# A branch on the number of chosen experts ahead of the loop over further experts

## The chip, the core and the metric

The kernel runs on one core of one Trainium2 chip. A core has a matrix engine (PE), a vector engine (DVE), an activation engine (ACT), a general engine (POOL) and an engine that here only starts transfers (SP). Each has its own instruction stream, and they meet through semaphores alone. The metric is the device time of one execution in microseconds; the comparison is made on the median of several executions.

## The reference

The input has 2 x 512 tokens of 1024 values. A first block adds a quantised product with a context. A second block, a mixture of experts with a shared expert, follows. Cut to what matters here:

```python
scores = softmax(xt @ router_w + router_b) + router_bias      # 1024 tokens x 16 experts
g = scores.reshape(T, 4, 4)
_, gidx = top_k(g.max(axis=-1), 2)                            # the 2 best groups of 4
masked = where(keep(gidx), g, -inf).reshape(T, 16)
_, idx = top_k(masked, 2)                                     # the 2 best experts of a token
gate = zeros((T, 16)).at[arange(T)[:, None], idx].add(vals)   # vals: the scores chosen
for e in range(16):
    h = silu(xt @ ew1[e] + eb1[e]) * (xt @ ew2[e] + eb2[e])   # 1024 -> 256
    y += gate[:, e:e+1] * (h @ ew3[e] + eb3[e])               # 256 -> 1024
z = silu(xt @ sw1 + sb1) * (xt @ sw2 + sb2) @ sw3 + sb3       # the shared expert, 1024 -> 512 -> 1024
x = x + tanh(g_ffn) * (y + z)
```

`xt` is the normalised token. `router_bias` is drawn once from the seed and multiplied by 6.017. Worked out from the reference's `setup_inputs()`, its 16 values are, group by group:

```
group 0 (experts 0 to 3)     -3.742    3.759   10.121   -4.862
group 1 (experts 4 to 7)    -14.238    5.391    8.802   -3.583
group 2 (experts 8 to 11)     7.276    8.880  -10.495   -2.829
group 3 (experts 12 to 15)   -4.648   -5.839   12.613    1.406
```

## The kernel before

All 1024 tokens stay in SBUF as 8 tiles of 128 tokens (`X`, `NT = 8`), transposed in `XT`, as a high and a low f16 part. Every product is made of three f16 products (high x high, high x low, low x high). The program does the quantised product first, then the shared expert, then the router, which finds out on the chip which experts any token chose: `nexp` holds their number, `EL` their indices, `sel` a one-hot row for each place in that list. Each engine reads `nexp` into a register with `chosen(engine)` (line 242).

Two of the chosen experts (`SLOTS = TOPK = 2`) are always there and have code of their own, written out: `expert_up` for 8 units (line 1325, two 128-row pieces of 256 x two halves of the tokens x two experts), whose results go through ACT (`eu_silu`, line 594), POOL (`gate_unit`, line 425, multiplication with the gate), DVE (`eu_gate`, line 872, which counts up `eu_hf`) and again ACT and DVE (high and low part, `eu_hi`, `eu_lo`, line 878). DVE also adds bias rows to `X` (`finish_rows`, lines 890 to 892).

If more than two experts were chosen, a loop `Fori(SLOTS, n)` takes the further ones, with register `a` from 2 to n - 1. It stands in each engine's code. One turn of it:

- SP reads the expert's index from `EL`, loads two bias columns, a bias row, the up weights in 8 pieces and the down weights (lines 312 to 328). It enters the loop only when `w3_lo`, `rows_fin` and `eu_hf >= 8` are reached.
- DVE makes the gate column from `sel[a]`, splits it into two f16 parts and builds diagonal matrices (lines 847 to 1058). PE turns them into gate rows (line 1338). ACT and DVE split the weights (lines 578, 860).
- PE does the up product, 192 matmuls (line 1349), unit by unit with ACT, POOL and DVE (lines 639, 435, 1067, 642, 1071), then the down product, 96 matmuls in 8 tiles (line 1362). DVE adds each tile into `X` (lines 1080, 1082). All of them wait for `xd_read` at the end of a turn.

The loop has its test at its end: the counter is raised and compared after the body. After it PE does the down products of the two fixed experts, and for the second half of the tokens those of the shared expert (`tile_down`, line 1385, 288 matmuls); DVE adds them to `X` (`tile_out`, line 901) and SP writes each tile out (line 368).

The order of work is the order in which the code is written, engine by engine; no scheduler is involved. On PE, line 1333 waits for `eu_hf >= 8` ahead of the loop; ACT waits there for `eu_done >= 8`. DVE and POOL go from `chosen` straight to the loop. The list index `a` beyond the number of chosen experts finds no one-hot row in `sel`, so the gate column is zero there.

Of the kernel before, what the change touches and what calls it, by code (L numbers as in the profile page):

```python
# [5 lines left out]
ALU = mybir.AluOpType  # L6
ACT = mybir.ActivationFunctionType
AX = mybir.AxisListType.X

P = 128  # L10
# [28 lines left out]
def build(nc, x, ctx_in, g_xattn, g_ffn, x1_scale, x1_zp, x2_scale, x2_zp, router_w, router_b, router_bias,  # L39
# [5 lines left out]
    with es:  # L45
# [200 lines left out]
        def _(sp):  # L246
# [59 lines left out]
            def expert_of(j):  # L306
                return sp.value_load(EL[0:1, bass.ds(j, 1)], min_val=0, max_val=E - 1)
# [40 lines left out]
            sp.wait_ge(w3_lo, 2 * SLOTS)  # L348
            sp.wait_ge(rows_fin, NT)
            sp.wait_ge(eu_hf, 8)  # L350
            with sp.Fori(SLOTS, n) as a:
                e = expert_of(a)
                sp.wait_ge(xw3_lo, 2 * a - 4)
                sp.sem_inc(further, 1)
                sp.wait_ge(xd_read, 8 * a - 16)
                sp.sem_inc(further, 1)
                load_bias_columns(e, SLOTS, xb_in)
                load_row(e, 1, xb_in)
                for q in range(4):
                    load_up_quarter(e, q, xw_in[q])  # L360
                sp.wait_ge(xw_lo, 4 * a - 4)
                sp.sem_inc(further, 1)
                load_down(e, 0, xw3_in)

            for i in range(NT):
                if i < NT - 1:
# [11 lines left out]
        def _(pool):  # L378
# [48 lines left out]
            for u in range(8):  # L427
                gate_unit(u)
            n = chosen(pool)
            with pool.Fori(SLOTS, n) as a:  # L430
                pool.wait_ge(xg_rdy, 2 * a - 2)
                pool.sem_inc(further, 1)
                for u in range(4):
                    pool.wait_ge(xu_silu, 4 * a - 8 + u + 1)
                    nc.gpsimd.tensor_tensor(SA[:, u % 2, :], SA[:, u % 2, :], GR[:, 0, u // 2, :], ALU.mult)\  # L435
                        .then_inc(xu_gated, 1)

        @block.scalar
        def _(act):  # L440
# [184 lines left out]

            n = chosen(act)
            act.wait_ge(eu_done, 8)
            with act.Fori(SLOTS, n) as a:
                act.wait_ge(xd_done, 8 * a - 16)
                act.sem_inc(further, 1)  # L630
                for q in range(4):
                    split_up_quarter(xw_in[q], 32 * a - 32, xw_hi, 0, q)
                for b in range(B):
                    gate_rows(b, xg_done, 2 * a - 4 + b + 1, GR[:, 0, b, :], xg_rdy)
                act.wait_ge(xb_in, 48 * a - 48)
                act.sem_inc(further, 1)
                for u in range(4):
                    act.wait_ge(xu_done, 4 * a - 8 + u + 1)
                    nc.scalar.activation(SA[:, u % 2, :], PS[:, 4 + 2 * (u % 2), :], ACT.Silu,
                                         bias=ebc[:, SLOTS, 0, u % 2:u % 2 + 1], scale=1.0 / UPS).then_inc(xu_silu, 1)  # L640
                    act.wait_ge(xu_hf, 4 * a - 8 + u + 1)
                    nc.scalar.activation(HX[:, 0, u % 2, u // 2 * S:(u // 2 + 1) * S], SA[:, u % 2, :], ACT.Copy,
                                         scale=HS / UPS).then_inc(xu_hi, 1)
                    act.wait_ge(xu_lo, 4 * a - 8 + u + 1)
                    act.sem_inc(further, 1)
                act.wait_ge(xw3_in, 16 * a - 16)
                for q in range(HC):
                    nc.scalar.activation(W3X[:, 0, q, :], W3F[0][:, q, :], ACT.Copy, scale=WS).then_inc(xw3_hi, 1)

        @block.vector
        def _(dve):
# [387 lines left out]
                    finish_rows(i)  # L1040

            n = chosen(dve)
            with dve.Fori(SLOTS, n) as a:
                count = [0]

                def linked(ins):

                    count[0] += 1
                    ins.then_inc(x_chain, 1)
                    dve.wait_ge(x_chain, XLINKS * a - SLOTS * XLINKS + count[0])  # L1050

                gate_column(SLOTS, sel[:, bass.ds(a, 1), :], linked)
                ins = split_gates(slice(SLOTS, SLOTS + 1), linked)
                ins.then_inc(xg_split, 1)
                dve.wait_ge(xg_split, a - 1)
                for h in range(2):
                    for b in range(B):
                        v.tensor_tensor(DGX[:, h, b, :, :], idh[:, :].unsqueeze(1).to_broadcast([P, TB, P]),
                                        gsp[:, h, SLOTS, b * TB:(b + 1) * TB].unsqueeze(2).to_broadcast([P, TB, P]),
                                        ALU.mult).then_inc(xg_diag, 1)  # L1060
                for q in range(4):
                    low_quarter(xw_hi, 4 * a - 8 + q + 1, 0, q, xw_lo)
                dve.wait_ge(xb_in, 48 * a - 48)
                linked(v.tensor_scalar(ebu[:, SLOTS, :], ebc[:, SLOTS, 1, :], UPS, None, ALU.mult))
                for u in range(4):
                    dve.wait_ge(xu_gated, 4 * a - 8 + u + 1)
                    v.scalar_tensor_tensor(SA[:, u % 2, :], PS[:, 5 + 2 * (u % 2), :], ebu[:, SLOTS, u % 2:u % 2 + 1],  # L1067
                                           SA[:, u % 2, :], ALU.add, ALU.mult).then_inc(xu_hf, 1)
                    dve.wait_ge(xu_hi, 4 * a - 8 + u + 1)
                    ts = slice(u // 2 * S, (u // 2 + 1) * S)  # L1070
                    v.scalar_tensor_tensor(HX[:, 1, u % 2, ts], SA[:, u % 2, :], HS / UPS, HX[:, 0, u % 2, ts], ALU.mult,
                                           ALU.subtract).then_inc(xu_lo, 1)
                for q in range(HC):
                    dve.wait_ge(xw3_hi, 2 * a - 4 + q + 1)
                    v.scalar_tensor_tensor(W3X[:, 1, q, :], W3F[0][:, q, :], WS, W3X[:, 0, q, :], ALU.mult,  # L1075
                                           ALU.subtract).then_inc(xw3_lo, 1)
                for i in range(NT):
                    Xi = X[:, i, :].rearrange("p (h n) -> p h n", h=2)
                    dve.wait_ge(xd_done, 8 * a - 16 + i + 1)
                    linked(v.scalar_tensor_tensor(Xi, PS[:, 2 * (i % 2):2 * (i % 2) + 2, :], cf[:, 11:12], Xi, ALU.mult,  # L1080
                                                  ALU.add))
                    v.scalar_tensor_tensor(X[:, i, :], B3[1], tgate[:, SLOTS, i:i + 1], X[:, i, :], ALU.mult, ALU.add)\  # L1082
                        .then_inc(xd_read, 1)
                dve.wait_ge(xd_read, 8 * a - 8)
                assert count[0] == XLINKS

            for i in range(NT):
                tile_out(i)
# [3 lines left out]
        def _(pe):  # L1092
# [238 lines left out]

            n = chosen(pe)
            pe.wait_ge(eu_hf, 8)
            with pe.Fori(SLOTS, n) as a:
                pe.wait_ge(xg_diag, 4 * a - 4)
                for b in range(B):
                    for h in range(2):
                        last = mm(PS[:, b, :], onesh[:, :], DGX[:, h, b, :, :].rearrange("p t n -> p (t n)"),
                                  start=(h == 0), stop=(h == 1))
                    last.then_inc(xg_done, 1)  # L1340
                pe.wait_ge(xw_lo, 4 * a - 4)
                for u in range(4):
                    if u >= 2:
                        pe.wait_ge(xu_hf, 4 * a - 8 + u - 1)
                    for w in range(2):
                        cs = slice(w * INTER + u % 2 * P, w * INTER + (u % 2 + 1) * P)
                        for k in range(KC):
                            for m, (wp, xp) in enumerate(((0, 0), (0, 1), (1, 0))):
                                last = mm(PS[:, 4 + 2 * (u % 2) + w, :], W12S[0][:, wp, k, cs],  # L1349
                                          XT[:, xp, k, u // 2 * S:(u // 2 + 1) * S], start=(k == 0 and m == 0),  # L1350
                                          stop=(k == KC - 1 and m == 2))
                    last.then_inc(xu_done, 1)
                pe.wait_ge(xu_lo, 4 * a - 4)
                pe.wait_ge(xw3_lo, 2 * a - 2)
                pe.wait_ge(xg_rdy, 2 * a - 2)
                for i in range(NT):
                    if i >= 2:
                        pe.wait_ge(xd_read, 8 * a - 16 + i - 1)
                    for h in range(2):
                        for c in range(HC):  # L1360
                            for m, (hp, wp) in enumerate(((0, 0), (1, 0), (0, 1))):
                                last = mm(PS[:, 2 * (i % 2) + h, :], HX[:, hp, c, i * P:(i + 1) * P],  # L1362
                                          W3X[:, wp, c, h * 512:(h + 1) * 512], start=(c == 0 and m == 0),
                                          stop=(c == HC - 1 and m == 2))
                    last.then_inc(xd_done, 1)
                pe.wait_ge(xd_read, 8 * a - 8)

            def tile_down(i):

# [50 lines left out]
```

## Time and profile before

| | us |
|---|---|
| median of 3 runs (lowest, highest) | 428.83 (427.85, 429.19) |
| the profiled execution: its own time | 426.34 |
| its span, first to last instruction | 424.5 |
| PE busy / DVE busy / ACT busy / POOL busy | 372.4 / 227.6 / 119.3 / 40.9 |
| mean granted TensorE clock | 0.964 of full speed |

The span is 1.84 us shorter than the profiled execution's own time, and that is 2.49 us below the median of the three timed runs. PE is busy for 88% of the span, and the core's 16 DMA engines move 90 GB/s in the mean. Read the table of stages first, then the queue instructions of the loop's lines, and only then the groups by line: the program has one stage whose work depends on the data.

### The profile page before, as it was taken

How to read it: one execution, taken by the hardware profiler on the slowest of the kernel's cores; microseconds unless marked ns; L12 is line 12 of the kernel's file. 1: busy time of each engine (PE TensorE's matmuls, PEld its weight loads, DVE VectorE, ACT ScalarE, POOL GpSimd, SP SyncE). 2: the span in 40 equal slices, each digit the busy share in tenths (PEclk: the TensorE clock that was granted, in tenths of full speed). 3: DMA queues.
4: the chain of work that ended last, by engine and by line, in shares of the span. 5: the costliest groups of instructions: out<-in, count | busy, mean ns of one | idle time of the engine just before them, and what ended most of it. 6: DMA issues, size and time to landing. Idle time of an engine off the chain costs nothing.

```text
span 424.5 us, 5372 instructions
## 1 busy us (share of the span) xinstructions
PE 372.4 (88%) x2191; PEld 181.9 (43%) x2191; DVE 227.6 (54%) x371; ACT 119.3 (28%) x133; POOL 40.9 (10%) x45
## 2 busy tenths in 40 slices
PE   0697998999999999999999993179993897999996
PEld 0343896444446444444444441024441342444442
DVE  4778879679845677245434898521112595221111
ACT  3893675882431116321231111221113000000000
POOL 2101101001300053011111111001111000000000
PEclk9999999999999999999999998569999798999999
DMA  8991504980560029250000000820000000121111
GB/s 305 379 314 28 171 30 135 236 300 0 100 148 2 2 78 323 96 198 2 0 0 2 0 0 2 247 99 2 2 0 0 0 2 1 63 111 59 60 56 49
DMA packets 37125, 38.19 MB, mean 90 GB/s; under 512 B 16740, under 2 KB 31084, under 8 KB 37100
## 3 DMA queue, kind: packets, MB, share of 16 engines
q1 hardware_dynamic: 37088, 37.85, 28.7%
q8 instruction: 17, 0.28, 0.3%
q14 instruction: 8, 0.07, 0.0%
q10 hardware_dynamic: 12, 0.00, 0.0%
HBM read 30.50 MB, written 4.19 MB: 82 GB/s over the span
## 4 chain that ended last, share of the span: by engine, by line
PE 62%; DVE 16%; issue 13%; ACT 3%; DMA 3%; POOL 2%; SPq 1%; ACTq 0%; POOLq 0%; DVEq 0%
PE PS L1385 15%; PE PS L1164 15%; PE PS L1325 15%; PE PS L1111 5%; PE PS L1199 5%; PE PS L1362 4%; DVE stats L666 3%; DMA ring<-in_L_ffn_ew_dram 1%; DVE areaW L720 1%; DVE X L891 1%; DVE X L1082 1%; DVE X L1080 1%; DVE X L890 1%; POOL SA L435 1%; DVE X L892 1%
## 5 line engine op out<-in xcount | busy, mean ns | idle before, releaser
L1164 PE MATMUL PS<-areaT,areaW 128*128 128x512 f16 x288 | 62.7, 379 | 1.4 <-DVE SA L751 1.4
L1349 PE MATMUL PS<-areaT,area 128*128 128x512 f16 x192 | 43.8, 393 | 8.3 <-DVE area L860 8.3
L1164 PEld LDWEIGHTS PS<-areaT,areaW 128*128 128x128 f16 x288 | 27.9, 98 | 35.0 <-DVE SA L751 1.6
L1325 PE MATMUL PS<-areaT,area 128*128 128x512 f16 x192 | 41.6, 379 | 0.0
L1325 PE MATMUL PS<-areaT,areaW 128*128 128x512 f16 x192 | 41.6, 379 | 0.0
L901 DVE SCALAR_TENSOR_TENSOR X<-PS,cf,X 128x512 f32<-128x512 f32 x16 | 12.0, 751 | 53.2 <-PE PS L1385 53.2
L1349 PEld LDWEIGHTS PS<-areaT,area 128*128 128x128 f16 x192 | 19.3, 101 | 33.3 <-DVE area L860 9.2
L1111 PE MATMUL PS<-area,areaQ 128*128 128x512 f16 x128 | 31.2, 395 | 0.3
L1362 PE MATMUL PS<-areaW 128*128 128x512 f16 x96 | 23.4, 404 | 8.3 <-DVE areaW L1075 7.9
L1325 PEld LDWEIGHTS PS<-areaT,areaW 128*128 128x128 f16 x192 | 18.8, 98 | 22.6
L1325 PEld LDWEIGHTS PS<-areaT,area 128*128 128x128 f16 x192 | 18.8, 98 | 22.6
L1385 PE MATMUL PS<-areaW,rows 128*128 128x512 f16 x96 | 22.6, 400 | 3.0 <-DVE X L1082 3.0
L1067 DVE SCALAR_TENSOR_TENSOR SA<-PS,ebu,SA 128x512 f32<-128x512 f32 x4 | 3.0, 752 | 39.5 <-POOL SA L435 39.5
L398 POOL TENSOR_TENSOR lnR<-lnV,mhalf 128x1 f32<-128x1 f32 (+1 forms) x13 | 13.4, 1034 | 100.3 <-DVE lnV L669 100.3
L666 DVE BATCH_NORM_STATS2 stats<-X 128x6 f32<-128x512 f32 x32 | 20.5, 683 | 4.2 <-DMA X<-in_x_dram 4.0
L1385 PE MATMUL PS<-SW,areaH 128*128 128x512 f16 x96 | 22.0, 379 | 0.0
L1385 PE MATMUL PS<-areaW,QI 128*128 128x512 f16 x96 | 22.0, 379 | 0.0
L1199 PE MATMUL PS<-SW,areaH 128*128 128x512 f16 x96 | 20.9, 379 | 0.0
L872 DVE SCALAR_TENSOR_TENSOR SA<-PS,ebu,SA 128x512 f32<-128x512 f32 x8 | 6.0, 748 | 25.8 <-POOL SA L425 25.8
L425 POOL TENSOR_TENSOR SA<-SA,areaQ 128x512 f32<-128x512 f32 x8 | 10.9, 1367 | 87.1 <-ACT SA L594 87.1
L1111 PEld LDWEIGHTS PS<-area,areaQ 128*128 128x128 f16 x128 | 12.4, 100 | 15.6 <-DVE area L703 1.3
L1362 PEld LDWEIGHTS PS<-areaW 128*128 128x128 f16 x96 | 9.3, 103 | 22.3 <-DVE areaW L1075 8.4
(174 smaller groups left out, 464.2 us busy)
## 6 DMA issues: line engine op xcount, KB each, us to landing
ring<-in_L_ffn_sw_dram SPq DMA_DIRECT2D x12, 512.0 KB, 5.0
ring<-in_L_ffn_ew_dram SPq DMA_DIRECT2D x24, 256.0 KB, 5.5
X<-in_x_dram SPq DMA_DIRECT2D x8, 512.0 KB, 6.2
areaT<-in_ctx_dram SPq DMA_DIRECT2D x8, 512.0 KB, 10.1
ring<-in_ctx_dram SPq DMA_DIRECT2D x8, 512.0 KB, 3.8
out_dram<-X SPq DMA_DIRECT2D x7, 512.0 KB, 2.6
ring<-in_L_ffn_ew_dram SPq DMA_DIRECT2D x3, 1024.0 KB, 4.9
B3b<-in_L_ffn_eb_dram SPq DMA_DIRECT2D x2, 512.0 KB, 6.2
```

Of the source, the lines that this page charges most:

```text
L398: nc.gpsimd.tensor_tensor(lnR[:, lo:lo + n], lnV[:, lo:lo + n], mhalf[:, 0:n], ALU.pow)\
L425: nc.gpsimd.tensor_tensor(SA[:, u % 2, :], SA[:, u % 2, :], GR[:, j, b, :], ALU.mult).then_inc(eu_gated, 1)
L666: ins = v.bn_stats(stats[:, i, 6 * h:6 * h + 6], X[:, i, h * 512:(h + 1) * 512])
L872: v.scalar_tensor_tensor(SA[:, u % 2, :], PS[:, EU_BANK[u] + 1, :], ebu[:, j, u % 2:u % 2 + 1], SA[:, u % 2, :], ALU.add, ALU.mult).then_i ...
L901: v.scalar_tensor_tensor(X[:, i, hs], PS[:, pb + h, :], cf[:, 11:12], X[:, i, hs], ALU.mult, ALU.add)\
L1111: mm(PS[:, AT_BANK[i] + h, :], Q1T[:, i % TB, k, :], Q2[:, k, h * 512:(h + 1) * 512], start=(k == 0), stop=False)
L1164: last = mm(PS[:, SU_BANK[half * SC + c] + w, lo:hi], SW[:, wp, 2 * c + w, k, :], XT[:, xp, k, tk], start=(k == 0 and n == 0), stop=(k == ...
L1199: last = mm(PS[:, pb + h, :], HT[:, hp, c, i * P:(i + 1) * P], SW3[:, wp, c, hs], start=(c == 0 and n == 0), stop=(c == SC - 1 and n == 2))
L1325: last = mm(PS[:, EU_BANK[u] + w, :], W12S[j][:, wp, k, cs], XT[:, xp, k, b * S:(b + 1) * S], start=(k == 0 and n == 0), stop=(k == KC - 1 ...
L1349: last = mm(PS[:, 4 + 2 * (u % 2) + w, :], W12S[0][:, wp, k, cs], XT[:, xp, k, u // 2 * S:(u // 2 + 1) * S], start=(k == 0 and m == 0), st ...
L1362: last = mm(PS[:, 2 * (i % 2) + h, :], HX[:, hp, c, i * P:(i + 1) * P], W3X[:, wp, c, h * 512:(h + 1) * 512], start=(c == 0 and m == 0), s ...
L1385: last = mm(PS[:, DN_BANK[i] + h, :], ht[:, hp, q, ts], w3[:, wp, c, hs], start=(s == 0 and m == 0), stop=(s == len(parts) - 1 and m == 2))
```

## The change

On each of the five engines the loop is put inside an `If(n > SLOTS)`. Nothing in the loop's body, ahead of it or behind it is changed. The same edit on PE, SP, POOL, ACT and DVE (`...` stands for the body, which is only indented):

```diff
@@ sync
             sp.wait_ge(w3_lo, 2 * SLOTS)
             sp.wait_ge(rows_fin, NT)
             sp.wait_ge(eu_hf, 8)
-            with sp.Fori(SLOTS, n) as a:
-                e = expert_of(a)
...
+            with sp.If(n > SLOTS):
+                with sp.Fori(SLOTS, n) as a:
+                    e = expert_of(a)
...
@@ gpsimd
             n = chosen(pool)
-            with pool.Fori(SLOTS, n) as a:
-                pool.wait_ge(xg_rdy, 2 * a - 2)
...
+            with pool.If(n > SLOTS):
+                with pool.Fori(SLOTS, n) as a:
+                    pool.wait_ge(xg_rdy, 2 * a - 2)
...
@@ scalar
             n = chosen(act)
             act.wait_ge(eu_done, 8)
-            with act.Fori(SLOTS, n) as a:
...
+            with act.If(n > SLOTS):
+                with act.Fori(SLOTS, n) as a:
...
@@ vector
             n = chosen(dve)
-            with dve.Fori(SLOTS, n) as a:
...
+            with dve.If(n > SLOTS):
+                with dve.Fori(SLOTS, n) as a:
...
@@ tensor
             n = chosen(pe)
             pe.wait_ge(eu_hf, 8)
-            with pe.Fori(SLOTS, n) as a:
-                pe.wait_ge(xg_diag, 4 * a - 4)
...
+            with pe.If(n > SLOTS):
+                with pe.Fori(SLOTS, n) as a:
+                    pe.wait_ge(xg_diag, 4 * a - 4)
...
```

In PE's instruction stream this is what stands where the loop is entered, before (an ISA row is a register operation; line 1325 is the last up product of the fixed experts, 1338 and 1349 are the loop's body):

```order
L1325 MATMUL PS<-areaT,areaW 128x512 x47
L242 TENSOR_LOAD nexp [waits el_rdy]
L242 ISA x2
L1334 UNCONDITIONAL_BRANCH [waits eu_hf]
L1334 ISA
L1338 MATMUL PS<-areaQ,onesh 128x512 [waits xg_diag]
```

and with the change (each line number of PE is 4 or 5 higher):

```order
L1329 MATMUL PS<-areaT,areaW 128x512 x47
L242 TENSOR_LOAD nexp [waits el_rdy]
L242 ISA x2
L1338 COMPARE_AND_BRANCH [waits eu_hf]
L1339 UNCONDITIONAL_BRANCH
L1339 ISA
L1343 MATMUL PS<-areaQ,onesh 128x512 [waits xg_diag]
```

A compare-and-branch has come in front of the way into the loop. It waits for the same semaphore as the old first instruction there.

Where PE leaves the loop, before (1362 is the body's down product, 1385 `tile_down`):

```order
L1362 MATMUL PS<-areaW 128x512 x11
L1366 REGISTER_ALU
L1334 REGISTER_ALU [waits xd_read]
L1334 COMPARE_AND_BRANCH
L1385 MATMUL PS<-areaW,rows 128x512 [waits w3_lo,eu_lo,eu_hf]
```

and with the change:

```order
L1367 MATMUL PS<-areaW 128x512 x11
L1371 REGISTER_ALU
L1339 REGISTER_ALU [waits xd_read]
L1339 COMPARE_AND_BRANCH
L1338 UNCONDITIONAL_BRANCH
L1390 MATMUL PS<-areaW,rows 128x512 [waits w3_lo,eu_lo,eu_hf]
```

Behind the loop's own test stands the jump to the end of the `If`; `tile_down` is that end.

## Rows read from the trace of the kernel before

**Rows 1.** Stages: busy us and count of each engine, granted clock, DMA share, GB/s

```profile
0.00:258.93 258.93, 239.31 (x1611) 124.37 (x1611) 173.69 (x312) 105.54 (x116) 34.30 (x40) 1.00 0.39 117
258.93:263.04 4.11, 0.00 (x0) 0.00 (x0) 4.04 (x3) 0.69 (x2) 1.51 (x1) 0.97 0.00 0
263.04:278.77 15.73, 1.89 (x4) 0.43 (x4) 9.20 (x15) 5.83 (x7) 0.00 (x0) 0.50 0.59 168
278.77:322.60 43.83, 43.81 (x192) 19.27 (x192) 4.36 (x7) 3.95 (x6) 3.79 (x3) 0.95 0.07 25
322.60:330.51 7.91, 0.00 (x0) 0.00 (x0) 3.81 (x4) 3.32 (x4) 1.26 (x1) 0.82 0.00 0
330.51:357.23 26.72, 23.36 (x96) 9.36 (x97) 20.51 (x16) 0.00 (x0) 0.00 (x0) 0.93 0.00 1
357.23:424.50 67.27, 64.01 (x288) 28.48 (x288) 12.02 (x16) 0.00 (x0) 0.00 (x0) 0.97 0.16 63
```

**Rows 2.** PE's sequencer at line 1334: duration ns min/median/max, first and last start

```profile
L1334 PEldq MOVE  x1: 33/33/33, 263.0 to 263.0; - x1
L1334 PEldq FUSED_REGOPS  x1: 50/50/50, 263.1 to 263.1; - x1
L1334 PEldq ALU_OP  x1: 32/32/32, 356.9 to 356.9; - x1
L1334 PEldq COMPARE_BRANCH  x1: 98/98/98, 357.0 to 357.0; - x1
```

**Rows 3.** Timeline from 255 us: start, us, engine, line, tile, idle and releaser

```profile
262.27 0.74 DVE L872 SCALAR_TENSOR_TENSOR SA<-PS,ebu,SA 128x512 f32<-128x512 f32 x1
263.70 0.69 DVE L878 SCALAR_TENSOR_TENSOR QI<-SA,QI 128x512 f16<-128x512 f32 x1 [0.70 <-ACT QI L600]
```

**Rows 4.** Chain that ended last, where the loop is left: start, us, what

```profile
355.55 1.30 DVE X L1082
356.85 0.38 issue
357.23 64.02 PE PS L1385 x288
421.25 0.02 issue
421.28 0.75 DVE X L901
```

**Rows 5.** The page: busy us and counts; instruction fetches (packets, MB, share of 16 engines)

```profile
PE 372.4 (88%) x2191; PEld 181.9 (43%) x2191; DVE 227.6 (54%) x371; ACT 119.3 (28%) x133; POOL 40.9 (10%) x45
...
q8 instruction: 17, 0.28, 0.3%
q14 instruction: 8, 0.07, 0.0%
```

**Rows 6.** The list of DMAs: count, KB each, us to landing

```profile
ring<-in_L_ffn_ew_dram SPq DMA_DIRECT2D x24, 256.0 KB, 5.5
...
ebc<-in_L_ffn_eb_dram SPq DMA_DIRECT2D x6, 1.0 KB, 2.2
```

**Rows 7.** Stages as in Rows 1, cut where the granted clock changes

```profile
278.77:283.26 4.49, 4.49 (x11) 1.64 (x12) 0.03 (x1) 0.00 (x0) 0.00 (x0) 0.50 0.67 234
330.51:334.46 3.95, 3.95 (x10) 1.47 (x11) 0.00 (x0) 0.00 (x0) 0.00 (x0) 0.50 0.00 0
357.23:358.35 1.12, 1.12 (x6) 0.53 (x7) 0.00 (x0) 0.00 (x0) 0.00 (x0) 1.00 0.02 7
358.35:361.76 3.41, 3.41 (x10) 1.18 (x9) 0.27 (x1) 0.00 (x0) 0.00 (x0) 0.50 0.00 0
```

**Rows 8.** DVE's and SP's sequencers at their loop lines, as in Rows 2

```profile
L1043 DVEq MOVE  x1: 50/50/50, 264.6 to 264.6; - x1
L351 SPq COMPARE_BRANCH  x1: 62/62/62, 279.4 to 279.4; - x1
```

**Rows 9.** Timeline behind the loop: the first evacuation and the first write

```profile
361.49 0.75 DVE L901 SCALAR_TENSOR_TENSOR X<-PS,cf,X 128x512 f32<-128x512 f32 x1 [4.65 <-PE PS L1385]
365.08 0.37 SPq L368 DMA_DIRECT2D out_dram<-X  x1
```

More of the change, by code:

```diff
@@ L350, in _ @@
             sp.wait_ge(eu_hf, 8)
-            with sp.Fori(SLOTS, n) as a:
-                e = expert_of(a)
[L353 to L363, printed above, removed]
+            with sp.If(n > SLOTS):
+                with sp.Fori(SLOTS, n) as a:
+                    e = expert_of(a)
+                    sp.wait_ge(xw3_lo, 2 * a - 4)
+                    sp.sem_inc(further, 1)
+                    sp.wait_ge(xd_read, 8 * a - 16)
+                    sp.sem_inc(further, 1)
+                    load_bias_columns(e, SLOTS, xb_in)
+                    load_row(e, 1, xb_in)
+                    for q in range(4):
+                        load_up_quarter(e, q, xw_in[q])
+                    sp.wait_ge(xw_lo, 4 * a - 4)
+                    sp.sem_inc(further, 1)
+                    load_down(e, 0, xw3_in)
             for i in range(NT):
@@ L429, in _ @@
             n = chosen(pool)
-            with pool.Fori(SLOTS, n) as a:
-                pool.wait_ge(xg_rdy, 2 * a - 2)
[L432 to L436, printed above, removed]
+            with pool.If(n > SLOTS):
+                with pool.Fori(SLOTS, n) as a:
+                    pool.wait_ge(xg_rdy, 2 * a - 2)
+                    pool.sem_inc(further, 1)
+                    for u in range(4):
+                        pool.wait_ge(xu_silu, 4 * a - 8 + u + 1)
+                        nc.gpsimd.tensor_tensor(SA[:, u % 2, :], SA[:, u % 2, :], GR[:, 0, u // 2, :], ALU.mult)\
+                            .then_inc(xu_gated, 1)
         @block.scalar
@@ L627, in _ @@
             act.wait_ge(eu_done, 8)
-            with act.Fori(SLOTS, n) as a:
[L629 to L644, printed above, removed]
-                    act.sem_inc(further, 1)
-                act.wait_ge(xw3_in, 16 * a - 16)
-                for q in range(HC):
-                    nc.scalar.activation(W3X[:, 0, q, :], W3F[0][:, q, :], ACT.Copy, scale=WS).then_inc(xw3_hi, 1)
@@ new lines, in _ @@
+            with act.If(n > SLOTS):
+                with act.Fori(SLOTS, n) as a:
+                    act.wait_ge(xd_done, 8 * a - 16)
+                    act.sem_inc(further, 1)
+                    for q in range(4):
+                        split_up_quarter(xw_in[q], 32 * a - 32, xw_hi, 0, q)
+                    for b in range(B):
+                        gate_rows(b, xg_done, 2 * a - 4 + b + 1, GR[:, 0, b, :], xg_rdy)
+                    act.wait_ge(xb_in, 48 * a - 48)
+                    act.sem_inc(further, 1)
+                    for u in range(4):
+                        act.wait_ge(xu_done, 4 * a - 8 + u + 1)
+                        nc.scalar.activation(SA[:, u % 2, :], PS[:, 4 + 2 * (u % 2), :], ACT.Silu,
+                                             bias=ebc[:, SLOTS, 0, u % 2:u % 2 + 1], scale=1.0 / UPS).then_inc(xu_silu, 1)
+                        act.wait_ge(xu_hf, 4 * a - 8 + u + 1)
+                        nc.scalar.activation(HX[:, 0, u % 2, u // 2 * S:(u // 2 + 1) * S], SA[:, u % 2, :], ACT.Copy,
+                                             scale=HS / UPS).then_inc(xu_hi, 1)
+                        act.wait_ge(xu_lo, 4 * a - 8 + u + 1)
+                        act.sem_inc(further, 1)
+                    act.wait_ge(xw3_in, 16 * a - 16)
+                    for q in range(HC):
+                        nc.scalar.activation(W3X[:, 0, q, :], W3F[0][:, q, :], ACT.Copy, scale=WS).then_inc(xw3_hi, 1)
@@ L1042, in _ @@
             n = chosen(dve)
-            with dve.Fori(SLOTS, n) as a:
[L1044 to L1085, printed above, removed]
@@ new lines, in _, with linked @@
+            with dve.If(n > SLOTS):
+                with dve.Fori(SLOTS, n) as a:
+                    count = [0]
+                    def linked(ins):
+                        count[0] += 1
+                        ins.then_inc(x_chain, 1)
+                        dve.wait_ge(x_chain, XLINKS * a - SLOTS * XLINKS + count[0])
+                    gate_column(SLOTS, sel[:, bass.ds(a, 1), :], linked)
+                    ins = split_gates(slice(SLOTS, SLOTS + 1), linked)
+                    ins.then_inc(xg_split, 1)
+                    dve.wait_ge(xg_split, a - 1)
+                    for h in range(2):
+                        for b in range(B):
+                            v.tensor_tensor(DGX[:, h, b, :, :], idh[:, :].unsqueeze(1).to_broadcast([P, TB, P]),
+                                            gsp[:, h, SLOTS, b * TB:(b + 1) * TB].unsqueeze(2).to_broadcast([P, TB, P]),
+                                            ALU.mult).then_inc(xg_diag, 1)
+                    for q in range(4):
+                        low_quarter(xw_hi, 4 * a - 8 + q + 1, 0, q, xw_lo)
+                    dve.wait_ge(xb_in, 48 * a - 48)
+                    linked(v.tensor_scalar(ebu[:, SLOTS, :], ebc[:, SLOTS, 1, :], UPS, None, ALU.mult))
+                    for u in range(4):
+                        dve.wait_ge(xu_gated, 4 * a - 8 + u + 1)
+                        v.scalar_tensor_tensor(SA[:, u % 2, :], PS[:, 5 + 2 * (u % 2), :], ebu[:, SLOTS, u % 2:u % 2 + 1],
+                                               SA[:, u % 2, :], ALU.add, ALU.mult).then_inc(xu_hf, 1)
+                        dve.wait_ge(xu_hi, 4 * a - 8 + u + 1)
+                        ts = slice(u // 2 * S, (u // 2 + 1) * S)
+                        v.scalar_tensor_tensor(HX[:, 1, u % 2, ts], SA[:, u % 2, :], HS / UPS, HX[:, 0, u % 2, ts], ALU.mult,
+                                               ALU.subtract).then_inc(xu_lo, 1)
+                    for q in range(HC):
+                        dve.wait_ge(xw3_hi, 2 * a - 4 + q + 1)
+                        v.scalar_tensor_tensor(W3X[:, 1, q, :], W3F[0][:, q, :], WS, W3X[:, 0, q, :], ALU.mult,
+                                               ALU.subtract).then_inc(xw3_lo, 1)
+                    for i in range(NT):
+                        Xi = X[:, i, :].rearrange("p (h n) -> p h n", h=2)
+                        dve.wait_ge(xd_done, 8 * a - 16 + i + 1)
+                        linked(v.scalar_tensor_tensor(Xi, PS[:, 2 * (i % 2):2 * (i % 2) + 2, :], cf[:, 11:12], Xi, ALU.mult,
+                                                      ALU.add))
+                        v.scalar_tensor_tensor(X[:, i, :], B3[1], tgate[:, SLOTS, i:i + 1], X[:, i, :], ALU.mult, ALU.add)\
+                            .then_inc(xd_read, 1)
+                    dve.wait_ge(xd_read, 8 * a - 8)
+                    assert count[0] == XLINKS
@@ L1333, in _ @@
             pe.wait_ge(eu_hf, 8)
-            with pe.Fori(SLOTS, n) as a:
-                pe.wait_ge(xg_diag, 4 * a - 4)
[L1336 to L1366, printed above, removed]
@@ new lines, in _ @@
+            with pe.If(n > SLOTS):
+                with pe.Fori(SLOTS, n) as a:
+                    pe.wait_ge(xg_diag, 4 * a - 4)
+                    for b in range(B):
+                        for h in range(2):
+                            last = mm(PS[:, b, :], onesh[:, :], DGX[:, h, b, :, :].rearrange("p t n -> p (t n)"),
+                                      start=(h == 0), stop=(h == 1))
+                        last.then_inc(xg_done, 1)
+                    pe.wait_ge(xw_lo, 4 * a - 4)
+                    for u in range(4):
+                        if u >= 2:
+                            pe.wait_ge(xu_hf, 4 * a - 8 + u - 1)
+                        for w in range(2):
+                            cs = slice(w * INTER + u % 2 * P, w * INTER + (u % 2 + 1) * P)
+                            for k in range(KC):
+                                for m, (wp, xp) in enumerate(((0, 0), (0, 1), (1, 0))):
+                                    last = mm(PS[:, 4 + 2 * (u % 2) + w, :], W12S[0][:, wp, k, cs],
+                                              XT[:, xp, k, u // 2 * S:(u // 2 + 1) * S], start=(k == 0 and m == 0),
+                                              stop=(k == KC - 1 and m == 2))
+                        last.then_inc(xu_done, 1)
+                    pe.wait_ge(xu_lo, 4 * a - 4)
+                    pe.wait_ge(xw3_lo, 2 * a - 2)
+                    pe.wait_ge(xg_rdy, 2 * a - 2)
+                    for i in range(NT):
+                        if i >= 2:
+                            pe.wait_ge(xd_read, 8 * a - 16 + i - 1)
+                        for h in range(2):
+                            for c in range(HC):
+                                for m, (hp, wp) in enumerate(((0, 0), (1, 0), (0, 1))):
+                                    last = mm(PS[:, 2 * (i % 2) + h, :], HX[:, hp, c, i * P:(i + 1) * P],
+                                              W3X[:, wp, c, h * 512:(h + 1) * 512], start=(c == 0 and m == 0),
+                                              stop=(c == HC - 1 and m == 2))
+                        last.then_inc(xd_done, 1)
+                    pe.wait_ge(xd_read, 8 * a - 8)
```

## The prediction

> **What bounds the kernel now.** I read the stages first. Up to 258.93 us PE is busy for 239.31 us at full clock, and after 357.23 us for 64.01 of 67.27 us [rows 1]. Between them lies everything that the diff wraps: 94.19 us from 263.04 to 357.23, with PE busy for 1.89 + 43.81 + 23.36 = 69.06 us and idle for the rest. Its matmul counts are 4, 192 and 96, and that is one turn of the loop (gate rows, up product, down product), no more and no less.
>
> Next come PE's sequencer rows at the loop's line. The counter is set once, at 263.0 us, and the compare-and-branch is passed once, at 357.0 us, behind the body [rows 2]; the chain goes on from there with `tile_down` [rows 4]. In the instruction order of before, no comparison stands ahead of the body: it is entered whatever n is. So one turn in the trace means n = 3, or n = 2 and a turn that nobody asked for. The trace cannot tell these apart; the inputs can.
>
> A score is a softmax value (0 to 1) plus the bias. Group 3's best is at least 12.61. Group 0's is at least 10.12, group 2's at most 8.88 + 1 = 9.88, group 1's at most 8.80 + 1. So each token keeps groups 3 and 0, whatever its logits. In them expert 14 has at least 12.61 and expert 2 at least 10.12, the next (expert 1) at most 3.76 + 1. All 1024 tokens choose experts 14 and 2. The narrowest margin is 0.24, far above f16 rounding. n is 2, and the turn in the trace works with a gate of zero: it reads weights of some expert and adds zeros to X.
>
> **The change, part by part.** With n = 2 the new comparison sends every engine past the loop. What goes is the whole turn: on PE 292 matmuls, on SP its 12 transfers, on ACT, POOL and DVE their share. The body works on tiles that it alone fills (or adds zeros to X), so nothing behind it needs it. The time that goes is not a sum of busy times but the distance between two moments on PE.
>
> *Start of the gap.* PE's last up product ends at 258.93. Its wait for eu_hf >= 8, which stays, is ended by DVE's line 872, 262.27 + 0.74 = 263.01 [rows 3]; PE's sequencer moves at 263.04 [rows 1, 2]. These 4.11 us of idle time remain.
>
> *The branch.* Between the start of the old compare-and-branch (about 356.97; it takes 98 ns) and the first matmul of `tile_down` at 357.23 lie 0.26 us [rows 2, 4]. The same at the new place: 263.04 + 0.26 = 263.30. In the trace that branch falls through, the new one is taken.
>
> *The jump.* The trace has no taken forward jump, so I bound it. The queue of instruction fetches moved 0.28 MB in 17 packets, 16.5 KB each; for 17 packets 0.3% of 16 engines' 424.5 us is 20.4 us, 1.2 us each [rows 5]. PE has 2191 loads and 2191 matmuls [rows 5], so a packet stands for some 257 instructions (4382 / 17). The body has 292 x 2 = 584 plus a few waits: the target lies over two packets ahead. If it is on the engine already, the jump costs about 0. If one packet must be fetched, PE stands still for the way of a small transfer from issue to landing, 2.2 us [rows 6], or up to that plus the packet's own 1.2 us, 3.4 us. Two such fetches one after the other are 6.8 us, my upper end. I take 2.8 us, the middle of one fetch, since the old body ran through by steady fetches and nothing announces the jump. PE then starts again at 263.30 + 2.8 = 266.10.
>
> The Trainium skill bears on this ("Runtime: NRT & Kernel Launch", Instruction fetch mechanics): prefetch is sequential, and "a taken branch whose target isn't in the current 2-page window forces a DMA fetch of the target page". By that rule, with pages of 256 instructions, 584 ahead is a miss; it gives no price. The same section gives TensorE room for 2048 instructions; were all of it filled ahead, there would be no miss. No row here shows which it is, so the jump at no cost is a rival below.
>
> *The tail.* From the first matmul of line 1385 to the end of the span it is 67.27 us [rows 1]. Every wait in it is met earlier or in the same order: eu_hf, eu_lo and w3_lo of the fixed experts are reached by 263.70 + 0.69 = 264.39 [rows 3], and the waits on y_rdy follow DVE's evacuations. DVE reads nexp and comes to its branch at 264.6 [rows 8]; the first result comes 361.49 - 357.23 = 4.26 us after the first matmul [rows 9], about 270.4 now. DVE, whose body is far shorter than PE's, has 5.7 us for its own jump. SP branches at about 263.1 and its first write comes 365.08 - 357.23 = 7.85 us after PE's start [rows 9]; that hides its jump. ACT and POOL have nothing left to do. If this cover were gone, DVE would have 4 tiles of PSUM banks to catch up in.
>
> *The clock.* The tail of before ran at 0.50 (1.2 GHz) for 3.41 us, after an idle time of 3.0 us; the two restarts with over 7 us of idle before them ran at 0.50 for 4.49 and 3.95 us [rows 7, 1]. Now PE idles for 266.10 - 258.93 = 7.2 us. I take the mean of those two, 4.2 us; 0.8 us more at half speed cost 0.4 us. Tail: 67.7 us.
>
> *Sum.* Span 266.10 + 67.7 = 333.8 us, against 424.5: 90.7 less. Against the profiled execution's own time that is 426.34 - 90.7 = 335.6; the median of the timed runs stands 2.49 us higher, 428.83 - 90.7 = 338.1 us. I predict 338.1.
>
> **The rivals.**
>
> *The jump is free.* For it: fetches run ahead in the body without a gap in the matmuls. Against it: the distance, over two packets. PE starts at 263.30, idle for 4.4 us. With the tail at 67.7 the span is 331.0 and the time 335.3. If the clock has not fallen either (in stage 258.93 to 263.04 it was still 0.97 in the mean, so it fell only at its end [rows 1]), the tail loses the half of 3.41 us: 65.6 us, span 328.9, time 333.2.
>
> *The jump is dear.* Two fetches in a row, or one that waits for others: 6.8 us, span 263.30 + 6.8 + 67.7 = 337.8, time 342.1.
>
> *The loop is not skipped, and nothing changes.* This needs n >= 3 in the runs that are timed, other inputs than the ones I worked out, or a chip whose list of experts is longer. The trace would look just as it does. Then the new rows cost two branches per engine on the path, 0.2 us: 429.0. The margins above speak against it.
>
> *Not skipped, and slower.* The same case, with the body left by the new jump at its end (the row behind the loop's test in the order of after). If that one, taken to the very next block, throws away what was fetched ahead, PE stands for one fetch of 2.8 us at 357 us, where nothing covers it: 428.8 + 0.2 + 2.8 = 431.8. It is slower as soon as that jump costs over 1.1 us.
>
> **How the numbers follow.** One fetch at PE's jump (PE back at 265 to 267.5): 0.58, 337 to 339.6, likeliest 338.1. Free jump: 0.27, 333.2 to 336. Dear jump: 0.10, up to 342.1. Not skipped: 0.03 with no change, 0.02 slower. The range of 334.0 to 341.0 leaves out the lowest part of the free jump (0.05), the top of the dear one (0.05) and the 0.05 of not skipped. A measurement of this kernel tells a difference from none at about 0.3%, 1.3 us. Faster 0.95, same 0.03, slower 0.02.
>
> **What would show it.** In the profile after: no instructions at the body's lines and 1899 matmuls in place of 2191; 24 - 8 = 16 transfers of 256 KB of expert weights in place of 24 [rows 6]; PE's compare-and-branch at about 263 us and the first matmul of `tile_down` at 266.1. That distance is the jump's price: 0.3 us means a free jump, 3.1 my forecast, over 5 the dear one. The stage from that matmul to the end should be 67.7 us, and DVE should wait for PE, never PE for DVE, in it. I am wrong if matmuls of the body's lines still appear, if DVE or SP comes out of its own jump later than PE needs it, or if the tail is over 1 us longer than before at the same clock.

## The result and the profile after

| | before | after |
|---|---|---|
| median (lowest, highest), us | 428.34 (426.86, 429.19), 4 runs | 337.41 (337.24, 338.44), 4 runs |
| ratio, 95% interval | 1 | 0.7885 (0.7857 to 0.7914) |
| the profiled execution: time, span | 426.34, 424.5 | 337.24, 335.4 |

The change makes the kernel 90.9 us faster; 338.1 us were forecast, in a range of 334.0 to 341.0. The line numbers of the changed kernel are 1 to 5 higher: 1329 is the last up product of the fixed experts (1325 before), 1390 `tile_down` (1385), 904 `tile_out` (901).

The page of the changed kernel, the same lines as before:

```profile
span 335.4 us, 4614 instructions
...
PE 304.2 (91%) x1899; PEld 154.1 (46%) x1899; DVE 190.1 (57%) x331; ACT 106.8 (32%) x117; POOL 35.9 (11%) x41
...
q8 instruction: 16, 0.26, 0.3%
...
ring<-in_L_ffn_ew_dram SPq DMA_DIRECT2D x16, 256.0 KB, 5.4
```

1899 matmuls in place of 2191 and 16 transfers of expert weights in place of 24 [rows 5, 6]: the whole turn of the loop is gone.

The stages of the changed kernel, cut at the same events as [rows 1] (columns as there; the last up product ends at 260.45, `eu_hf` reaches 8 at 264.57, `tile_down` starts at 268.25, the clock rises at 271.53):

```profile
0.00:260.45 260.45, 240.24 (x1611) 125.60 (x1611) 173.31 (x312) 105.46 (x115) 34.35 (x40) 0.99 0.38 116
260.45:264.57 4.12, 0.00 (x0) 0.00 (x0) 4.04 (x3) 0.69 (x2) 1.50 (x1) 1.00 0.01 2
264.57:268.25 3.68, 0.00 (x0) 0.03 (x1) 0.69 (x1) 0.62 (x1) 0.00 (x0) 0.52 0.03 9
268.25:271.53 3.28, 3.28 (x8) 1.17 (x9) 0.00 (x0) 0.00 (x0) 0.00 (x0) 0.50 0.02 5
271.53:335.40 63.87, 60.65 (x281) 27.30 (x279) 12.01 (x16) 0.00 (x0) 0.00 (x0) 1.00 0.17 66
```

The stages of the loop, 94.19 us from 263.04 to 357.23 [rows 1], have become the 3.68 us of the third row. What PE's sequencer did in it (line 1338, duration in ns):

```profile
L1338 PEldq COMPARE_BRANCH  x1: 3520/3520/3520, 264.6 to 264.6; - x1
```

The old branch, which fell through, took 98 ns [rows 2]. This one is taken and takes 3520. In the same 3.68 us the list of DMAs has one packet on the queue of instruction fetches that is PE's:

```profile
q8 instruction: 1, 0.02, 1.9%
```

1.9% of 16 engines' 3.68 us is 1.1 us of transfer. The packet starts 0.95 us after the branch does, and the branch ends 1.5 us after the packet: most of the 3.5 us is the way of the fetch, not its bytes. The same comparison on DVE (line 1046), one record of its line:

```profile
L1046 DVEq COMPARE_BRANCH  x1: 72/72/72, 266.1 to 266.1; - x1
```

SP's takes 53 ns, ACT's and POOL's 45 ns each. Only PE, whose jump goes over some 600 instructions (a matmul counts as two, its weight load and itself), stands still. And behind the jump (timeline of the changed kernel):

```profile
272.65 0.75 DVE L904 SCALAR_TENSOR_TENSOR X<-PS,cf,X 128x512 f32<-128x512 f32 x1 [6.73 <-PE PS L1390]
...
276.01 0.37 SPq L369 DMA_DIRECT2D out_dram<-X  x1
```

DVE waits for PE (6.73 us), not PE for DVE, and SP's first write comes 7.76 us after PE's start; before it was 7.85 [rows 9].

### The profile page after: what moved, and what is told of

The parts are those of the page before. It is cut to its first block, busy times and chain, and to the rows that moved or that the text cites. A ratio compares the mean times of both kernels' runs of the same rounds, so it can differ in the third digit from the quotient of the medians.

```text
span 335.4 us, 4614 instructions
## 1 busy us (share of the span) xinstructions
PE 304.2 (91%) x1899; PEld 154.1 (46%) x1899; DVE 190.1 (57%) x331; ACT 106.8 (32%) x117; POOL 35.9 (11%) x41
## 4 chain that ended last, share of the span: by engine, by line
PE 76%; DVE 14%; issue 4%; ACT 3%; DMA 1%; POOL 1%; ACTq 0%; DVEq 0%; POOLq 0%
PE PS L1390 19%; PE PS L1168 19%; PE PS L1329 19%; PE PS L1115 7%; PE PS L1203 6%; DVE stats L669 3%; PE PS L1184 3%; DVE X L894 2%; DVE X L893 2%; DVE X L895 1%; DMA sc<-in_g_ffn_dram 1%; PE PS L1122 1%; DVE X L740 1%; POOL lnR L399 1%; DVE SA L875 1%
## 5 line engine op out<-in xcount | busy, mean ns | idle before, releaser
L1168 PEld LDWEIGHTS PS<-areaT,areaW 128*128 128x128 f16 x288 | 27.9, 98 | 35.0 <-DVE SA L754 1.6
L1329 PE MATMUL PS<-areaT,area 128*128 128x512 f16 x192 | 41.6, 379 | 0.0
L1329 PEld LDWEIGHTS PS<-areaT,area 128*128 128x128 f16 x192 | 18.8, 98 | 22.6
L1329 PEld LDWEIGHTS PS<-areaT,areaW 128*128 128x128 f16 x192 | 18.8, 98 | 22.6
L875 DVE SCALAR_TENSOR_TENSOR SA<-PS,ebu,SA 128x512 f32<-128x512 f32 x8 | 6.0, 748 | 25.8 <-POOL SA L426 25.8
L596 ACT ACTIVATE SA<-PS,ebc 128x512 f32<-128x512 f32 x8 | 5.5, 688 | 46.8 <-PE PS L1329 46.8
L1390 PEld LDWEIGHTS PS<-areaW,rows 128*128 128x128 f16 x96 | 9.7, 102 | 20.6 <-issue 10.5
L1184 PE MATMUL PS<-areaT,areaW 128*128 128x128 f16 x256 | 16.4, 229 | 1.2 <-issue 1.2
L1184 PEld LDWEIGHTS PS<-areaT,areaW 128*128 128x128 f16 x256 | 15.8, 103 | 1.4 <-issue 1.3
L487 ACT ACTIVATE rows<-X,lnB,lnA 128x1024 f32<-128x1024 f32 x8 | 9.9, 1239 | 19.9 <-DVE lnB L680 19.9
```

Of the source, the lines that this page charges most:

```text
L487: nc.scalar.activation(rows[:, i % 2, :], X[:, i, :], ACT.Identity, bias=lnB[:, i:i + 1], scale=lnA[:, i:i + 1]).then_inc(ln_xs, 1)
L875: v.scalar_tensor_tensor(SA[:, u % 2, :], PS[:, EU_BANK[u] + 1, :], ebu[:, j, u % 2:u % 2 + 1], SA[:, u % 2, :], ALU.add, ALU.mult).then_i ...
L1168: last = mm(PS[:, SU_BANK[half * SC + c] + w, lo:hi], SW[:, wp, 2 * c + w, k, :], XT[:, xp, k, tk], start=(k == 0 and n == 0), stop=(k == ...
L1184: mm(PS[:, 4 + 2 * c + w, tk], SW[:, 0, 2 * c + w, k, :], XT[:, xp, k, tk], start=(k == 0 and xp == 0), stop=False)
L1329: last = mm(PS[:, EU_BANK[u] + w, :], W12S[j][:, wp, k, cs], XT[:, xp, k, b * S:(b + 1) * S], start=(k == 0 and n == 0), stop=(k == KC - 1 ...
L1390: last = mm(PS[:, DN_BANK[i] + h, :], ht[:, hp, q, ts], w3[:, wp, c, hs], start=(s == 0 and m == 0), stop=(s == len(parts) - 1 and m == 2))
```

## The experiments

All of them were compared with the kernel before on the same chip. Theory A: the gain is the skipped turn, and the only price on the path is PE's jump, which has to fetch its target.

**1. No branch at all.** There is neither loop nor `If` on any of the five engines. Written as an edit of the kernel before (PE's part; `...` stands for the body, which is deleted too):

```diff
-            with pe.Fori(SLOTS, n) as a:
...
```

> The loop and the branch ahead of it are left out on all five engines (right for these inputs, where n is 2; experts beyond two would be missing). Theory A (PE's taken jump over the body fetches its target; nothing else in the branch is on the path): in the profile the gap between eu_hf >= 8 and the first matmul of tile_down falls from 3.68 us to about 0.3, and the time from 337.4 to 334.0. Rival B (the 3520 ns record is a wait or a restart of PE, not the jump): the gap stays at 3 us or more and the time at 337.4.

Measured: 333.96 us (332.34 to 334.65), ratio 0.7792 (0.7739 to 0.7844). Stages of this kernel, up to the end of the up product, the gap, and the rest:

```profile
0.00:259.46 259.46, 239.30 (x1611) 124.43 (x1611) 173.25 (x312) 105.29 (x115) 34.35 (x40) 1.00 0.38 117
259.46:263.63 4.17, 0.00 (x1) 0.01 (x1) 4.08 (x3) 0.71 (x2) 1.50 (x1) 0.92 0.00 0
263.63:330.50 66.87, 63.66 (x288) 28.43 (x288) 12.71 (x17) 0.60 (x1) 0.00 (x0) 0.98 0.16 63
```

The gap is 4.17 us, nearly all of it the wait for `eu_hf`. With the branch it is 4.12 + 3.68 = 7.80. The jump costs 3.6 us by the gaps and 3.4 by the medians, as expected. Rival B is refuted.

**2. No branch on PE alone.** The changed kernel with `If` and loop deleted on PE only.

> The loop and its branch are left out on PE alone; SP, ACT, POOL and DVE keep both (right for n = 2). Theory A: the same time as the kernel without any branch, 334.0 within 0.5, since the four other jumps lie beside PE's work. Rival C (one of the other jumps is as dear and DVE or SP is late for PE or for the writes): over 1 us above it, 335 to 337.4.

Measured: 333.98 us (333.24 to 335.28), ratio 0.7788 (0.7732 to 0.7845), the same as without any branch (333.96). The jumps of the other four engines cost nothing that can be measured, as theory A has it; rival C is refuted.

**3. The wait moved behind the branch.**

```diff
-            pe.wait_ge(eu_hf, 8)
             with pe.If(n > SLOTS):
+                pe.wait_ge(eu_hf, 8)
                 with pe.Fori(SLOTS, n) as a:
```

`tile_down` has waits of its own, so nothing is given up by this.

> PE's wait for eu_hf >= 8 moves from ahead of the branch into the branch's body, so that PE can jump while its queue still holds up products. Theory A (the price is a fetch, which needs only the sequencer): the branch starts at the end of the nexp load, 3.5 us before the queue is empty, the fetch is hidden, tile_down starts within 0.5 us of the last up product, 7.5 us earlier than in the changed kernel, and the clock doesn't fall, 1.6 us more: 328.3. Rival B (the price comes after the queue has run dry, so it can't be hidden): only the 4.1 us of wait go, 333.3.

Measured: 328.42 us (326.94 to 329.95), ratio 0.7665 (0.7604 to 0.7726). The jump is as long as before, but it starts at 256.6 us, while PE still has matmuls in its queue:

```profile
L1337 PEldq COMPARE_BRANCH  x1: 3320/3320/3320, 256.6 to 256.6; - x1
```

Stages of this kernel, as for experiment 1:

```profile
259.73:260.08 0.35, 0.00 (x1) 0.03 (x1) 0.35 (x1) 0.31 (x1) 0.00 (x0) 1.00 0.00 0
260.08:325.60 65.52, 62.32 (x288) 28.08 (x288) 16.36 (x20) 1.00 (x2) 1.52 (x1) 1.00 0.16 65
```

The gap of 7.80 us is 0.35, and the tail is 65.52 us in place of 67.15 (3.28 + 63.87 above), since the clock stays at 1.00 (2.4 GHz). Together 9.1 us, and the medians differ by 9.0. The fetch is still there, one packet on PE's fetch queue between 256.6 and 260.08 us, but it stops the sequencer only: the up products that PE had queued ran on until 259.73 us and covered 3.1 of the jump's 3.3 us.

**4. The jump announced.** A prefetch hint for it two units (96 matmuls) ahead:

```diff
             for u in range(8):
+                if u == 6:
+                    soon = pe.mark_branch_hint_location()
                 expert_up(u)
...
-            with pe.If(n > SLOTS):
+            jump = pe.br_cond(n > SLOTS, on_true="pe_further", on_false="pe_down")
+            jump.branch_hint(soon)
+            with nc.body("pe_further", valid_engines=PE_ONLY):
...
```

> PE's jump is announced: a branch prefetch hint stands two units (96 matmuls) ahead of it. Everything else is the changed kernel. Theory A: if the hint brings the target in beside the sequential fetches, the 3520 ns record falls to about 0.1 us and the time to 334.0. If the stall is no fetch (rival B), or the hint does nothing: 337.4 and a record of 3.5 us.

Measured: 334.26 us (332.26 to 335.65), ratio 0.7778 (0.7721 to 0.7835), and the record of the jump:

```profile
L1343 PEldq COMPARE_BRANCH  x1: 401/401/401, 265.6 to 265.6; - x1
```

**5. The loop entered through the `If`.** The condition is `n > SLOTS - 1` on each engine, so that the turn of zeros is run.

> The branch asks n > SLOTS - 1 on all five engines, so with n = 2 the loop is entered through the If and takes its one turn of zeros. Theory A (the gain is the turn that is skipped and nothing else; an If that is entered costs its few branches): the time of the kernel before, 428.5, within 1.3 us; PE's loop is left through one more jump of about 0.1 us. Rival D (the jump behind the loop's test throws away what was fetched ahead): 428.5 + 3.4 = 431.9.

Measured: 428.71 us (427.14 to 431.09) beside 428.37 of before, ratio 1.0029 (0.9998 to 1.0059). PE's leaving of the loop (duration in ns, start):

```profile
L1339 PEldq COMPARE_BRANCH  x1: 102/102/102, 359.9 to 359.9; - x1
```

The first matmul of `tile_down` follows at 360.18, 0.27 us later, as before (0.26). Rival D's 431.9 us would be a ratio of 1.008, above the interval: it is refuted. A cost of the entered `If` is not shown; the interval leaves room for up to 2.5 us. In the profiled executions the loop's stage is 1.39 us longer than before (95.58 us at a mean clock of 0.83, against 94.19 at 0.86) and the tail 1.65 us shorter (65.62 against 67.27), differences that go with the clock; at the branch itself the rows are as before.

**6 and 7. Shorter bodies.** The body on PE, which isn't run, is made shorter, so that the jump is shorter: an up product over one and over four of the eight row blocks.

```diff
-                            for k in range(KC):
+                            for k in range(1):
```

> In the body that is jumped over, PE's up product has 24 matmuls in place of 192 (right for n = 2, since the body isn't run): 124 matmuls and as many loads, some 262 instructions from jump to target, where the changed kernel has some 600. Theory A1 (what is on the engine is the packet being read and the next one): the target is in the next packet, the record falls to 0.1 us and the time to 334.0. Theory A2 (any taken jump of PE costs 3.5 us): 337.4.

> As the shorter body, with 96 matmuls in the up product: 196 matmuls, some 406 instructions from jump to target. The jump stands some 200 instructions into its packet of 256, so the target is in the second packet after it. Theory A1 (only the packet being read and the next are there): a record of 3.5 us, 337.4. If more than that is fetched ahead (A3): 0.1 us, 334.0.

Measured: 338.02 us (337.21, 338.83), ratio 0.7883 (0.7842 to 0.7923), for some 262 instructions; 338.25 (337.47, 339.04), ratio 0.7888 (0.7848 to 0.7928), for some 406. The two records of the jump, of the shorter and the longer body:

```profile
L1338 PEldq COMPARE_BRANCH  x1: 3297/3297/3297, 264.4 to 264.4; - x1
```

```profile
L1338 PEldq COMPARE_BRANCH  x1: 3880/3880/3880, 265.4 to 265.4; - x1
```

The longer one is as theory A1 has it. It takes 0.4 us more than the changed kernel's because its packet starts 1.46 us after the jump and not 0.95; why is not shown. The shorter one is a miss: A1 expected no stall. Either any taken jump costs this (A2), or my count of where the packets begin was off and its target lies in the second packet after all.

**8. Both edits of 3 and 4.**

> Both edits on PE: the wait moved into the branch's body and the hint two units ahead. Theory A: the fetch is hidden twice over; what the moved wait alone still shows between the last up product and tile_down (0.3 us) can't shrink by more than 0.2 us, so the same time as with the moved wait alone, 328.4, within 1.0. Rival: the hint's early fetch displaces a packet that is still needed, and PE stalls before the jump: 330 or more.

Measured: 327.13 us (326.50 to 328.50), ratio 0.7635 (0.7602 to 0.7668), the fastest version. Its jump starts at 256.7 us and takes 406 ns; the up product runs into `tile_down` without a gap, and the mean clock of the whole execution is 0.999. Against the moved wait alone (0.7665) the intervals overlap, so the hint's own share isn't shown.

**9 and 10. Two very short bodies**: two waits and no matmul; 52 matmuls.

> The shorter bodies (262 and 406 instructions from jump to target) still showed PE's record at 3.3 and 3.9 us, so the distance doesn't decide down to 262. Here PE's loop body holds two waits and no matmul (right for n = 2): the target is about 8 instructions behind the jump, in the same packet. Theory A4 (a taken jump stalls when its target lies outside the packet being read, even in the next one): a record near 0.1 us and 334.0. Theory A2 (any taken jump of PE costs 3.3 us or more): 3.3 us and 337.4.

> PE's loop body has 52 matmuls (right for n = 2): the target is about 111 instructions behind the jump. The fetches of the kernel before place the next packet's boundary some 28 instructions behind the jump, so the target is early in the next packet. A4: a record of 3.3 us, 337.4, as for 262 instructions. A2: the same. If it is instead the distance in instructions (A5: PE's queue holds what is near): 0.1 us, 334.0.

Measured: 334.25 us (333.74, 334.75), ratio 0.7805 (0.7775 to 0.7836), and 334.70 (333.98, 335.41), ratio 0.7816 (0.7774 to 0.7857). The record of the jump is the same in both; that of the body with 52 matmuls:

```profile
L1338 PEldq COMPARE_BRANCH  x1: 365/365/365, 265.3 to 265.3; - x1
```

So not every taken jump stalls (A2 falls), and the next packet is there already (A4 as written falls too). Left are packets (A4') or a reach of some length between 111 and 262 instructions (A5).

**11 and 12. Packet or distance.** The body with 100 matmuls; and the body with 124 that stalled, with the jump shifted against the packets:

```diff
             for u in range(8):
+                if u in (5, 6):
+                    for _ in range(30):
+                        pe.wait_ge(eu_hf, 1)
                 expert_up(u)
```

> PE's loop body has 100 matmuls (right for n = 2): the target is some 207 instructions behind the jump, 96 further than in the run with 52 matmuls (0.37 us, no stall) and 58 nearer than in the one with 124 (3.3 us). Theory A4' (what is on the engine is the packet being read and the next; the jump stands shortly before a boundary, so a target up to some 256 further on is there): a record near 0.37 us, 334.3. Theory A5 (a fixed reach of about 128 instructions): 3.3 us and 337.4.

> The body with 124 matmuls that stalled for 3.3 us, same distance from jump to target, but 60 waits that are met already stand ahead of it in PE's stream (30 each before the sixth and the seventh unit), so that the jump lies early in its packet and the target in the next one in place of the second. Theory A4' (packets decide): a record near 0.37 us and 334.3. Theory A5 (distance decides): 3.3 us again, 337.4. The added waits themselves lie behind PE's queue of matmuls, up to 1 us if they don't.

Measured: 334.19 us (334.16, 334.21), ratio 0.7793 (0.7770 to 0.7816), with a record of 365 ns; and 334.85 (333.89, 335.82), ratio 0.7809 (0.7753 to 0.7865), with this one:

```profile
L1341 PEldq COMPARE_BRANCH  x1: 457/457/457, 265.5 to 265.5; - x1
```

The 60 waits are 30 instructions in PE's stream, since two waits go into one: its trace has 30 semaphore records more than the changed kernel's, 2 of them at line 1322 and 28 at the added line:

```profile
L1336 PEldq EVENT_SEMAPHORE  x28: 51/51/51, 226.2 to 238.0; - x28
```

The body and the distance are those of experiment 6, and the record falls from 3297 to 457 ns because 30 instructions more stand ahead of it. The fetch queue shows why. In experiment 6 no packet moves for PE between 253 and 264 us, and one moves inside the jump. With the shift, one moves between 253 and 256 us, 11 us ahead of the jump:

```profile
q8 instruction: 1, 0.02, 1.8%
```

The distance does not decide; where the packets begin does. A fixed reach of 128 is refuted by experiment 11 as well.

These counts also place the jump. A target some 207 instructions on is there and one some 262 on is not, so in the unshifted kernels the jump stands within the last few instructions of its packet of 256. The boundaries that experiments 7 and 10 were planned by, some 56 and 28 instructions behind the jump, were wrong: with either, the target of experiment 6 would have been in the next packet. And the target of experiment 9, 8 instructions on, was then in the next packet too, not in the jump's own as its plan says. A target in the jump's own packet was not tested.

## Why the prediction was right

*That there was a turn to skip* was right: n is 2, argued from the biases with a margin of 0.24, and the loop before ran once all the same, because its test stands at its end. The counts of the changed kernel show it, and experiment 5 shows the other side: the same turn behind an entered `If` gives the old time back.

*Start of the gap*: 4.12 us of idle time, 4.11 forecast. It came 1.53 us later in the span than before (264.57 against 263.04), which I had not forecast. In this execution the clock stood at half speed for 3.42 us early on. The stage 42.83 to 46.25 us of the changed kernel and then of the one before, where code and order are the same:

```profile
42.83:46.25 3.42, 3.12 (x30) 3.15 (x31) 3.35 (x6) 2.45 (x3) 0.55 (x1) 0.50 0.48 144
```

```profile
42.83:46.25 3.42, 3.14 (x57) 3.17 (x58) 3.35 (x6) 2.44 (x3) 0.56 (x1) 1.00 0.37 111
```

30 matmuls in place of 57 in the same busy time. Experiment 11, which has the same branch and the same code ahead of it, did not have this dip (clock 1.00 up to the jump, which starts at 263.3), so it isn't the change's. It is why the spans differ by 89.1 us and not by 90.7.

*Branch and jump*: 0.26 + 2.8 = 3.06 us forecast, 3.68 measured. The mechanism was right (one fetch of the target, shown by experiments 1 and 4), the size was 0.6 us low. I had taken the middle of 2.2 and 3.4 us; the end with the packet's own time in it was nearer. The jump also costs 0.37 us where nothing has to be fetched (experiments 9 to 11), and 0.10 of my 0.26 were for a branch that falls through. The rival of the free jump, at 0.27, would have given 333.2 to 336, and is what experiments 1 and 4 measured with the cause taken away.

The rule of the Trainium skill ("Runtime: NRT & Kernel Launch", Instruction fetch mechanics) that a taken branch whose target isn't in the current 2-page window has to fetch it agrees with PE here, as far as it was tested: targets in the next packet cost 0.37 to 0.46 us, those further on 3.3 to 3.9. The other case that the prediction kept open, a store filled far ahead in which the target would have been found, did not come true: a target some 262 instructions on was missing.

*The tail*: 67.7 us forecast, 67.15 measured, mainly because the clock was back after 3.28 us and not 4.2. Every wait in it was covered, as argued; the cover of DVE's and SP's jumps was not needed, since these took 72 and 53 ns.

*Sum*: 333.8 + 1.53 (the head) + 0.62 (the jump) - 0.55 (the tail) = 335.4 us, the measured span, 1.6 us above the forecast one. That the median came out 0.7 us below its forecast (337.4 against 338.1) is luck. I had added 2.49 us from the profiled execution to the median, as before; after the change these two lie only 0.17 us apart (337.24 and 337.41), and the 2.3 us that this takes away outweigh the 1.6. The mechanism was right; the closeness of the median is not to be credited to the terms.

## What to carry to other kernels

Read the counts of a data-dependent loop against its inputs: a loop with its test at the end runs once for an empty range, and here that one turn was a fifth of the time, with PE busy in it for 69 of 94 us, on products whose gate is zero. A branch over a long body cost next to nothing here once its sequencer reached it while the engine still had work queued, so put waits that only the skipped code needs inside the branch; 9 us more came from moving one line.

## What the runs showed of the hardware

PE's taken jump costs 0.37 us (three runs, 365 ns each) even when nothing has to be fetched for it, a branch that falls through 98 to 102 ns; the taken jumps of DVE, SP, ACT and POOL took 45 to 72 ns. A target beyond the next packet of instructions costs 3.3 to 3.9 us on PE: in the changed kernel 0.95 until its packet starts, 1.1 of transfer and 1.5 from there to the jump's end. A hint 96 matmuls ahead removes it (401 ns). Placement alone decides over 2.8 us: the same jump over the same distance took 3297 ns, and 457 with 30 instructions more ahead of it.
